# Two late slots of a four-layer metaformer take two steps per attention unit, and four multiplications of the third slot run on GpSimd

## The reference, cut to what matters

```python
# layer 2, token part: attention, 4 groups x 8 heads, each query keeps its 16 largest logits
x = x + (pos + pos_b[None, :, None]).transpose(0, 2, 1)
q, k, v = split(x @ qkv_w.T + qkv_b)
logits = einsum('bmd,bpd->bmp', q * scale, k);  _, idx = top_k(logits, 16)
attn = softmax(q . k[idx]);  out = sum(attn * v[idx]) @ wo_w.T + wo_b
# layer 3, convolutional part, after a layer norm over channels: Hadamard product, then 4-bit rounding
x_had = x @ H64;  std = sqrt(mean(x_had ** 2))            # one std per image
scale = 2.5139 * std + 1e-8;  step = 2 * scale / 15
xq = round(clip(x_had) / step + 0.5) * step - step * 0.5
# layer 3, token part, after a layer norm: 8 experts, the best 2, and a shared one
probs = softmax(x @ router);  combine = the two largest of each token
y = (silu(x @ W_gate[e]) * (x @ W_up[e])) @ W_down[e]
x = x + shared(x) + sum_e combine[:, e] * y[e]
```

## Time and profile before

| what | value |
|---|---|
| time, median of three runs | 897.02 us (894.5 to 898.59) |
| the profiled execution, its own time | 895.26 us |
| its span in the profile | 893.5 us |
| attention loop, first to last unit | from 566 us to 813.45 us |
| from the last unit's end to the span's end | 80.05 us |
| VectorE busy over the span | 567.2 us (63%) |
| TensorE busy over the span | 714.9 us (80%) |

### The profile page before, as it was taken

One profiled execution on the slowest core, in us unless ns is written; L12 is line 12 of the kernel. 1 busy time (PEld: TensorE's weight loads), 2 busy tenths in 40 slices (PEclk: granted clock), 3 DMA queues, 4 the chain that ended last, 5 costly groups with the idle time before them and its releaser, 6 DMA issues.

```text
span 893.5 us, 13790 instructions
## 1 busy us (share of the span) xinstructions
PE 714.9 (80%) x4364; PEld 570.7 (64%) x4364; DVE 567.2 (63%) x2170; ACT 336.4 (38%) x825; POOL 262.9 (29%) x323
## 2 busy tenths in 40 slices
PE   6996869899829999988859997788675676586768
PEld 5885769798617999975328884556454453353436
DVE  8989522113332551387962033899999999989774
ACT  1000524445503122211101212688685674564321
POOL 5104434212370000020220003555555534633200
PEclk9997989999959999998989999799897899998989
DMA  9802355656620356710002400000000002002020
GB/s 342 277 1 72 115 176 137 199 144 166 207 62 1 142 206 219 275 56 0 1 0 83 165 1 0 2 1 1 0 1 1 1 1 49 0 14 48 13 48 25
DMA packets 25846, 72.64 MB, mean 81 GB/s; under 512 B 2840, under 2 KB 11032, under 8 KB 22960
## 3 DMA queue, kind: packets, MB, share of 16 engines
q1 hardware_dynamic: 23728, 67.56, 23.4%
q0 software_dynamic: 2048, 4.20, 1.5%
HBM read 61.61 MB, written 10.14 MB: 80 GB/s over the span
## 4 chain that ended last, share of the span: by engine, by line
PE 50%; DVE 33%; issue 7%; POOL 5%; ACT 4%; DMA 0%; DVEq 0%; POOLq 0%; ACTq 0%
PE PB L1046 6%; PE PB L914 6%; PE PB L928 5%; PE PB L1255 5%; DVE X L2340 4%; DVE arena L2591 3%; DVE top L2602 3%; PE PB L842 3%; DVE top L2586 3%; DVE arena L2605 3%; PE PB L832 2%; PE PB L1433 2%; POOL arena L654 2%; DVE XT L1943 1%; PE PB L791 1%
## 5 line engine op out<-in xcount | busy, mean ns | idle before, releaser
L783 POOL TENSOR_TENSOR arena<-arena 128x512 f32<-128x512 f32 x64 | 81.3, 1271 | 121.8 <-ACT arena L1888 121.8
L1342 PE MATMUL PB<-ring 128*128 128x256 f32 x256 | 75.9, 424 | 18.1 <-ACT arena L1880 17.3
L587 POOL TENSOR_TENSOR lnrs<-lnve,mhalf 128x4 f32<-128x4 f32 x20 | 20.8, 1038 | 228.8 <-DVE lnve L1926 228.4
L1567 PE MATMUL PB<-w_first,arena 128*128 128x128 f32 x256 | 45.3, 305 | 51.1 <-POOL arena L783 50.7
L1629 ACT ACTIVATE arena<-PB,arena 128x128 f32<-128x128 f32 x212 | 59.9, 367 | 60.7 <-PE PB L914 54.0
L1888 ACT ACTIVATE arena<-arena,nmx 128x256 f32<-128x256 f32 x128 | 58.2, 506 | 58.2 <-DVE arena L2605 57.8
L1567 PEld LDWEIGHTS PB<-w_first,arena 128*128 128x128 f32 x256 | 31.5, 153 | 75.8 <-POOL arena L783 71.0
L914 PE MATMUL PB<-arena 128*128 128x128 f32 x424 | 60.7, 289 | 13.8 <-issue 11.7
L1342 PEld LDWEIGHTS PB<-ring 128*128 128x128 f32 x256 | 48.0, 208 | 30.3 <-issue 18.1
L914 PEld LDWEIGHTS PB<-arena 128*128 128x128 f32 x424 | 54.7, 202 | 16.4 <-issue 13.7
L928 PE MATMUL PB<-ring,arena 128*128 x424 | 60.0, 286 | 2.1 <-ACT arena L1629 1.1
(11 more groups left out here) (327 smaller groups left out, 1589.8 us busy)
## 6 DMA issues: line engine op xcount, KB each, us to landing
ring<-in_taps_dram SPq DMA_DIRECT2D x12, 1536.0 KB
arena<-in_experts_dram SPq DMA_DIRECT2D x53, 258.0 KB
ring<-in_taps_dram SPq DMA_DIRECT2D x7, 1792.0 KB
arena<-comb_rows SPq DMA_DIRECT2D x6, 512.0 KB, 5.9
w_later<-in_later_dram SPq DMA_DIRECT2D x1, 2951.5 KB, 14.7
rows_back<-arena SPq DMA_DIRECT2D x11, 256.0 KB
ring<-in_second_dram SPq DMA_DIRECT2D x1, 2048.0 KB, 19.0
rows_there<-arena SPq DMA_DIRECT2D x2, 960.0 KB, 21.5
```

The source lines that it names most:

```text
L783: g.tensor_tensor(PR[c % 2], E1[c % 2], E2[c % 2], ALU.subtract).then_inc(sub_ready, 1)
L1342: last = mm(PB[c % 2][:, q * 256:q * 256 + 256], QM[c // 2 % 3][:, o + P * q:o + P * q + P], Kc[:, N * s + HW * j:N * s + HW * j + HW], st ...
L1567: last = tr(PB[3][:, kt * 256 + q * P:kt * 256 + q * P + P], PR[c % 2][:, q * 256 + kt * P:q * 256 + kt * P + P], ident)
```

## The change

A table `QUICK = {1: 26, 2: 10}` and a function `due(k, c)` are new. For slots 0, 3 and 4 nothing changes: one step per turn. Slot 1 takes one step per turn up to step 26 (c = 58) and two from then on: steps 27 and 28 at c = 59, 37 and 38 at c = 64, 41 and 42 at c = 66. Slot 2 takes one up to step 10 (also c = 58) and then two: 11 and 12 at c = 59, 21 and 22 at c = 64, 31 and 32 at c = 69, 41 and 42 at c = 74. Every engine's loop calls `follow` for each of the steps due.

Slot 2's `combine` leaves DVE and becomes four POOL instructions at steps 38 to 41, each with the wait for `cb_in`. Its `down` moves from steps 38 to 40 to steps 42 to 44 and its last copy from 41 to 45. Waits follow the new order: the turns into PB[4], the router's bank of slot 2 (PB[5] in place of PB[2]), `gates(3, 3)`, and a wait of slot 3's `combine` for the four on POOL.

```diff
+QUICK = {1: 26, 2: 10}
+
+
+def due(k, c):
+    d = c - PARTS[k][2]
+    q = QUICK.get(k, UNITS + TAIL)
+    return (d,) if d <= q else (2 * d - q - 1, 2 * d - q)
...
+            def combine(k, i):
+                pool.wait_ge(cb_in, 32 * k + 32)
+                pool.wait_ge(gu_ready, 5 * k + i + 1)
+                pool.wait_ge(gus_ready, 4 * k)
+                g.tensor_tensor(GU[k % 2][i], GU[k % 2][i], CB[:, i, :], ALU.mult).then_inc(gus_ready, 1)
...
+                if k == 2 and 38 <= d <= 41:
+                    combine(k, d - 38)
...
                 for k in reversed(range(len(PARTS))):
-                    follow(k, c - PARTS[k][2])
+                    for d in due(k, c):
+                        follow(k, d)
...
+                    elif k == 3 and i == 3:
+                        pe.wait_ge(combT_ready, 2 * SLOTS + 3)
                     elif k == 3:
-                        pe.wait_ge([lg_read, lg_read, pt_ready, po_ready][i], [UNITS, UNITS, UNITS, 2 * SLOTS][i])
+                        pe.wait_ge([lg_read, lg_read, pt_ready][i], UNITS)
...
                 elif d == 10:
...
-                    elif k < 3:
+                    elif k < 4:
                         pe.wait_ge(*at(xn_ready[7], k))
-                    elif k == 3:
-                        pe.wait_ge(ms_ready, 3)
                     else:
-                        pe.wait_ge(*at(xn_ready[7], 3))
+                        pe.wait_ge(ms_ready, 4)
                     part_turn(6, k, PB[4])
...
                 if k < 3:
                     if d in (26, 28, 30, 32, 34):
                         gates(k, (d - 26) // 2)
-                    if d == 38:
+                    first = 42 if k == 2 else 38
+                    if d == first:
                         pe.wait_ge(gus_ready, 4 * k + 4)
                         pe.wait_ge(gu_ready, 5 * k + 5)
-                    if 38 <= d <= 40:
-                        down(k, 2 * d - 76, PB[6])
-                        down(k, 2 * d - 75, PB[6])
+                    if first <= d <= first + 2:
+                        down(k, 2 * (d - first), PB[6])
+                        down(k, 2 * (d - first) + 1, PB[6])
...
-                elif d == (41 if k < 3 else 36):
+                elif d == [41, 41, 45, 36, 36][k]:
                     final_copy(k, PB[6 if k < 3 else 4])
...
+                    dve.wait_ge(gus_ready, 12)
                     dve.wait_ge(cb_done, 4 * (k - 3) + i // 2 * 2 + 2)
...
-                    if 35 <= d <= 38:
+                    if k < 2 and 35 <= d <= 38:
                         combine(k, d - 35)
```

More of the change, by code:

```diff
@@ L1492, in follow @@
                 elif d == 24:
-                    if k < 2:
+                    if k < 3:
                         pe.wait_ge(ms_ready, k + 1)
-                    elif k < 4:
-                        pe.wait_ge(ms_ready, k + 2)
+                    elif k == 3:
+                        pe.wait_ge(ms_ready, 5)
                     else:
@@ L1500, in follow @@
                 elif d == 26:
-                    bank = PB[5 if k == 1 else 2]
-                    if k == 1:
-                        pe.wait_ge(po_ready, 7)
+                    bank = PB[5 if k in (1, 2) else 2]
+                    if k in (1, 2):
+                        pe.wait_ge(po_ready, k + 6)
                     elif k == 0:
                         pe.wait_ge(x_after_attn, 2)
-                    elif k == 2:
+                    elif k == 3:
                         pe.wait_ge(x_after_attn, 5)
@@ L1855, in follow @@
                 elif d == 31:
-                    comb_copy3(k, PB[5 if k == 1 else 2])
-                elif d == (41 if k < 3 else 36):
+                    comb_copy3(k, PB[5 if k in (1, 2) else 2])
+                elif d == [41, 41, 45, 36, 36][k]:
                     final_copy(k, PB[6 if k < 3 else 4])
@@ L1883, in _ @@
                 for k in reversed(range(len(PARTS))):
-                    follow_early(k, c - PARTS[k][2])
+                    for d in due(k, c):
+                        follow_early(k, d)
                 if c < UNITS:
@@ L2563, in follow @@
                 elif d == 28:
-                    router_start(2, k, some, PB[5 if k == 1 else 2])
+                    router_start(2, k, some, PB[5 if k in (1, 2) else 2])
                 elif d == 30:
@@ L2596, in _ @@
                 for part in reversed(range(len(PARTS))):
-                    follow(part, c - PARTS[part][2])
+                    for d in due(part, c):
+                        follow(part, d)
                 if c < UNITS:
```

## The result

The changed kernel takes 926.6 us (median of 4 runs, 924.79 to 937.97) against 897.3 us for the kernel before, timed beside it: a ratio of 1.039, 95% interval 1.033 to 1.044. It is slower by 29 us. Of each kernel a ratio counts only the single runs within 1.5% of its fastest, so it can differ by up to 0.3% from the quotient of the medians. The profiled execution took 924.79 us with a span of 922.9; before it was 895.26 with 893.5.

What follows compares the result with a forecast made beforehand. No engine bounds alone; TensorE and VectorE hand work to each other and wait by turns. Chained waits and work gave a span of 918.2, plus 5 for the clock and 1.8 around the span: 925.0 us, range 905 to 938.

Steps and rivals of the forecast that it cites:

- rival (a): Whole kernel: the new waits between engines chain as summed, giving 915 to 935 us; chance 0.76.
- Rival (c): Only unit 59's wait is new, +3.8 us, and gains take it back: 894.4 us, no change; chance 0.05.
- rival (d): VectorE bounds the last 80 us; units absorb the moved steps at bare price: 888.8 us; chance 0.09.
- The waits of unit 59: VectorE stands idle before `router_start` and the first `gated`: 5.75 and 1.2 us, +3.8 us over before.
- `mean_square` in unit 61: Slot 2's step between VectorE's halves waits 1.5 us for ACT's `had_copy` and PE's sum.
- `std` in unit 62: VectorE waits behind POOL's subtraction of unit 61: +1.4 us.
- The tanh waits: VectorE waits for ACT's tanh before `gated`: 0.2 us in unit 60, 2.0 us in unit 61.
- Two `combine` in the units: Work coming into VectorE's units 59 to 63, counted at 0.6 us each.
- Up to the end of `pv`: From the last unit's end, rounding, statistics, `combine` and slot 1's `down` ahead of `pv`: 9.9 us.
- The clock: PE runs at the lower clock after five new idle gaps: 0 to 8.4 us, 5 taken.
- The products on GpSimd: Slot 2's multiplications leave VectorE: 2.4 and 2.28 us saved go into waits; interference with VectorE taken as 0.
- The tail: Slot 4's chain from `pv` to the end: 74 to 79 us expected, 69.8 before.

Runs made afterwards that it cites:

- run 1: The changed kernel with slot 2's four `combine` back on VectorE, leaving only the doubled steps: 927.9 us, ratio 1.038 to the kernel before.
- run 4: The changed kernel with PE's last `pv` moved ahead of the slot steps of turn 64: 919.6 us, ratio 1.028 to the kernel before.
- run 8: The kernel before with PE's last `pv` moved ahead of the slot steps of turn 64: 896.2 us, ratio 1.005.
- run 2: The kernel before with slot 2's four `combine` on GpSimd at the same steps, no doubling: 896.2 us, ratio 1.004.
- run 3: The kernel before with slot 1 alone doubled, from unit 59: 906.9 us, ratio 1.012.
- runs 5: The kernel before with slots 1 and 2 doubled only from turn 65, products on VectorE: 904.1 us, ratio 1.012.
- 11: The kernel before with slot 1 doubled from turn 65 and slot 2 only from turn 75: 905.2 us, ratio 1.014.
- run 12: The kernel before with slot 1 alone doubled, from turn 65: 905.9 us, ratio 1.013.
- run 10: The kernel before with the eight small matmuls that spread slot weights split in two fours: 893.6 us, ratio 1.001.

## Why the prediction held, and where its terms were off

**The likeliest case was right.** The time is 926.6 against 925.0, the waits chain as in rival (a), and run 1 shows that the doubling makes the loss. Rival (c), no change, and rival (d), the units taking the steps at their bare price, fell at unit 59.

**Units 59, 61 and 62: right in size.** The waits of unit 59 were put at 5.75 and 1.2; they were 5.68 and 1.17. `mean_square` in unit 61 was put at 1.5 and waited 1.78; `std` in unit 62 at 1.4 and waited 1.45.

**The tanh waits: too small.** Unit 60 was put at 0.2 and waited 2.28 and 0.39. Unit 61 was put at 2.0 and waited 3.05 and 0.46. The steps took PE's products and gates at the upper clock; they ran at the lower, 1.91 instead of 1.02 for two matmuls. The prediction had entered the clock as one lump of 5 us at the end. It belongs to these terms. Together with the wait of 0.9 for unit 63, which did not come, this is 3 us of the 4.6 by which the last unit was late.

**Two `combine` in the units: too small.** They took 1.38 and 1.59 us instead of 0.69: 1.6 us more. The first began at 828.25 beside POOL's subtraction of unit 62, which ran from 827.81 to 829.08, and the second at 831.05 beside a piece of `add_rounded`, which ran from 830.83 to 832.09. The prediction looked for the quarrel between VectorE and POOL at slot 2's products and took 0 there. On the path it was at POOL's older work, beside which the doubling had put these `combine`.

**Up to the end of `pv`: 12.3 us, not 9.9.** `down(1, 0)` and `(1, 1)` took 3.78 at the lower clock, where the sum had 1.7. By run 4's profile this order costs 4.5 us, the price of placing `down` ahead of `pv`; the medians of the two kernels are 7.0 apart, and the profiles show 2.7 more in the units, from the clock.

**The clock: right in kind, too small.** Counted where it falls, it took some 8 us, an estimate from the rows: 1.9 in unit 60, 1.5 in unit 61, 2.0 in `down(1)` and 2.6 in `down(2)`. That is the prediction's upper end, 8.4, and not its 5. Its reading that the lower clock follows each idle time of 2.5 us and up does not hold in other profiles: 2.53 us of it stand ahead of logits in 1.10 us in run 4, and 2.51 ahead of eight `down` matmuls in 3.70 us, not 5.40, in run 8.

**The products on GpSimd: right in result.** The terms said that 2.4 and 2.28 us of VectorE would turn into waits; run 2 measures no gain. Beside the products two steps of `round4(3)` took 1.85 instead of 0.80 and 1.23 instead of 0.29, 2.0 us together. They cost nothing, as assumed: VectorE then waited 5.04 us for slot 4's sum. The Trainium skill (SBUF — State Buffer, "Who interferes with whom") states that of GpSimd and a VectorE instruction in a two-port mode the one that issues first has the ports for its whole length and the other is blocked. These rows agree with it; the upper end of 3.8 us that the prediction worked out by that rule did not reach the path.

**The tail: right.** From `pv` to the end 74 to 79 us were expected; it was 76.5. The terms without the clock gave 74.0, and the ten `down(2)` matmuls took 6.90 us where 4.3 were counted. `pv` was put near 844, up to 847 with the clock; it ended at 846.4. The last 16.0 us were 15.9. Some small slips in the sums change nothing: 1.7 + 1.9 was entered as 3.7, 5 x 1.7 is 8.5, and the ends of rival (a) add up to 932.7 us, not 935.

**What was luck.** From unit 59 on the change cost 34.2 us in the profile, where the terms and the clock gave 29.7. The number still fits because unit 59 began 4.8 us earlier than in the profile of before, in code that the change does not touch. In the fourteen profiles that start lies between 782.6 and 789.5, and that of before was near the top. Against a kernel before timed at 894.8 us, run 1, which ends at the same place after unit 59, was 33 us slower. The sum was made on one execution, and this spread belongs in its range as a term of its own.

**What stays open.** Slot 2's doubling costs two thirds of the loss when it begins at unit 59 (runs 1 and 3) and nothing measurable when it begins in the tail (runs 5, 11 and 12). Its waits in units 61 and 62 and its `round4` ahead of the last units, all before `pv`, fit that. Slot 1's third is the same whether it is doubled from unit 59 (run 3, 1.012) or in the tail (run 12, 1.013), so waits in the units need not be its cause. Slot 2 alone, doubled inside the units, was not run: begun at unit 59, its gates would stand on PE ahead of slot 1's last gates, which they wait for, and PE would stop; a start one turn later was not tried. Why the clock falls in some tails and not in others is open too. No version beat the kernel before.

## What to carry to other kernels

In a schedule where each engine works in a fixed order, the distance in turns between a producer and its consumer is what hides latency. Halving it can bring each latency out, on each engine that has other work behind the wait; that it need not is shown by slot 2, whose doubling in the tail cost nothing measurable. Before moving a step ahead, look at what stands behind it on every queue that it is moved past: here `down(1)` ahead of `pv` cost 4.5 us, and slot 1's steps doubled in the tail, with `down(1)` ahead of slot 4's first steps, some 8 us beside the clock, with the same instructions. And where a stall is added on PE, price the matmuls behind it at the lower clock, in the very term where they stand.

## What the runs showed of the hardware

VectorE and POOL lengthen each other's instructions. Tiny ones pay the most for their size: 0.17 us became 1.19 beside POOL's products (run 2). In the changed kernel a `combine` of 0.69 became 1.59, and POOL's own 1.27 became 1.72.

The granted clock can fall during work. In run 8 ten matmuls took 3.54 instead of 2.40 us with only 0.35 us of idle time before them, behind 2.6 us of small matmuls that run 10's kernel also has in two halves and the kernel before has unchanged. Over the fourteen profiles the same last work took about 15.9, 17.5 or 20.3 us. A gain of 3 us earlier in the program can be lost that way, so a variant must be judged by timed rounds and the clock of its tail, not by one trace.
